# Scores of two heads at a time in the row halves of TensorE, and another order of the opening, in a layer of attention plus mixture of experts on one core

## The reference

```
x = L0_attn_x
xn = _layernorm(x, axis=-1)
x = x + attention(xn) + ffn(xn)

# attention: 16 heads of D = 8
qkv = x @ Wqkv + bqkv
q = q * cos + rotate_half(q) * sin           # k the same
scores = einsum('bhtd,bhsd->bhts', q, k) / sqrt(D)
probs = softmax(scores, axis=-1)
attn = einsum('bhts,bhsd->bhtd', probs, v) ; attn @ Wout + bout

# ffn: one shared and 16 routed experts of inner width 64, the best 2 of each token
router_logits = sigmoid(x @ gate_w + gate_b)
expert_values, expert_indices = top_k(router_logits, k=2)   # values divided by their sum
hg, hu = x @ experts_wg[e], x @ experts_wu[e]
out[e] = (silu(hg) * hu) @ experts_wd[e]
return x + shared_mlp(x) + sum of the 2 selected, weighted
```

## Time and profile before

| what | value |
|---|---|
| median of 3 runs | 251.86 us |
| the profiled execution | 251.57 us |
| its span, first to last instruction | 249.8 us (1.8 us lie around it) |
| PE / DVE / ACT / POOL busy | 215.1 / 186.4 / 141.6 / 173.0 us |
| granted clock of TensorE, mean | 0.963 of 2.4 GHz |
| DMA, mean | 106 GB/s |

### The profile page before, as it was taken

How to read it: one execution, slowest core, us unless ns; L and a number is a source line. 1 busy time by engine, 2 the same in 40 slices (tenths; PEclk the granted TensorE clock), 3 DMA queues, 4 the chain that set the end, 5 groups by cost and what they waited for, 6 DMA issues and landing times.

```text
span 249.8 us, 4841 instructions
## 1 busy us (share of the span) xinstructions
PE 215.1 (86%) x1612; PEld 140.1 (56%) x1612; DVE 186.4 (75%) x400; ACT 141.6 (57%) x266; POOL 173.0 (69%) x247
## 2 busy tenths in 40 slices
PE   0473399997898999999858999999999999999973
PEld 0341165564555666676634566676767656675541
DVE  5885929999787687899935787998688878774301
ACT  2455033235556856675267567656666757667761
POOL 9186646899966748979195768778876774558622
PEclk9995559999999999999999999999999999999999
DMA  6925628120354331320744070504553540211201
GB/s 221 368 40 164 204 63 203 36 76 12 111 173 128 109 96 53 107 45 20 217 143 140 3 192 5 145 0 134 155 147 106 171 133 22 85 53 37 86 3 42
DMA packets 35953, 26.53 MB, mean 106 GB/s; under 512 B 4236, under 2 KB 30156, under 8 KB 35916
## 3 DMA queue, kind: packets, MB, share of 16 engines
q1 hardware_dynamic: 35224, 25.30, 34.8%
q10 hardware_dynamic: 704, 0.92, 1.0%
HBM read 18.53 MB, written 7.47 MB: 104 GB/s over the span
## 4 chain that ended last, share of the span: by engine, by line
PE 48%; DVE 21%; POOL 11%; issue 6%; DMA 5%; ACT 4%; SPq 4%; POOLq 0%; DVEq 0%; ACTq 0%
PE PV L514 8%; DVE mx L886 5%; PE S2b L500 4%; PE S2a L500 3%; PE S1a L486 3%; PE S1b L486 3%; PE Y L373 3%; PE FB L373 3%; SPq L302 3%; PE FA L373 3%; DMA wbc<-route_w 3%; POOL hid_lo L1001 2%; PE FA L375 2%; PE FA L374 2%; PE FB L375 2%
## 5 line engine op out<-in xcount | busy, mean ns | idle before, releaser
L1001 POOL TENSOR_TENSOR hid_lo<-gu,hid_hi 128x512 fp32r<-128x512 f32 (+1 forms) x36 | 46.4, 1288 | 26.6 <-ACT hid_hi L694 26.6
L661 ACT ACTIVATE probs<-S2b 128x512 f32<-128x512 f32 x64 | 38.1, 596 | 28.3 <-PE S2b L500 28.2
L985 POOL TENSOR_TENSOR gu<-gu,wbc 128x512 f32<-128x512 f32 x32 | 41.0, 1282 | 13.2 <-DMA wbc<-route_w 9.6
L886 DVE TENSOR_REDUCE mx<-S1a 128x2 f32<-128x512 f32 x65 | 44.4, 683 | 7.3 <-PE S1a L486 7.3
L886 DVE TENSOR_REDUCE mx<-S1b 128x2 f32<-128x512 f32 x63 | 43.0, 683 | 7.3 <-PE S1b L486 7.2
L661 ACT ACTIVATE probs<-S2a 128x512 f32<-128x512 f32 x64 | 38.3, 599 | 11.7 <-PE S2a L500 9.6
L514 PE MATMUL PV<-probs,vx 128*32 128x256 f32 x512 | 34.9, 384 | 4.3 <-ACT probs L661 4.3
L694 ACT ACTIVATE hid_hi<-gu 128x512 fp32r<-128x512 f32 (+1 forms) x36 | 22.7, 632 | 24.6 <-POOL gu L985 23.1
L895 DVE SCALAR_TENSOR_TENSOR th<-th,FA 128x512 f32<-128x512 f32 (+1 forms) x36 | 24.5, 682 | 13.7 <-ACT th L673 13.2
L673 ACT ACTIVATE th<-FA 128x512 f32<-128x512 f32 (+1 forms) x36 | 21.5, 597 | 18.5 <-PE FA L375 18.2
L876 DVE TENSOR_TENSOR gu<-FB,th 128x512 f32<-128x512 f32 (+1 forms) x36 | 24.6, 683 | 5.5 <-PE FB L375 5.4
(11 more groups left out here) (129 smaller groups left out, 433.1 us busy)
## 6 DMA issues: line engine op xcount, KB each, us to landing
wbc<-route_w SPq DMA_DIRECT2D x64, 128.0 KB, 3.1
q_hat<-q_parts SPq DMA_DIRECT2D x32, 96.0 KB, 2.8
k_hat<-k_parts SPq DMA_DIRECT2D x32, 96.0 KB, 2.7
k_parts<-parts SPq DMA_DIRECT2D x8, 192.0 KB, 2.2
q_parts<-parts SPq DMA_DIRECT2D x8, 192.0 KB, 2.2
x_sb<-in_x SPq DMA_DIRECT2D x4, 256.0 KB, 4.0
q_parts<-parts SPq DMA_DIRECT2D x8, 128.0 KB, 2.1
k_parts<-parts SPq DMA_DIRECT2D x8, 128.0 KB, 2.1
```

The source lines that it names most:

```text
L661: nc.scalar.activation(probs[:, head % (2 * NQ), :], S2[head % 2][:], ACT.Exp, scale=SCALE).then_inc(exp_done, 1)
L886: nc.vector.tensor_reduce(mx[:, (q // QB) % 2, (q // 2) % 2, :, q % 2, i], S1[use % 2][:].rearrange("p (t s) -> p t s", t=SB), axis=AX.X, ...
L985: nc.gpsimd.tensor_tensor(gu[:, m % 2, :], gu[:, m % 2, :], wbc[:, g % 2, c - 1, :], ALU.mult).then_inc(gu_weighted, 1)
L1001: nc.gpsimd.tensor_tensor(hid_lo[0:rows, m % 2, :], gu[0:rows, m % 2, :], hid_hi[0:rows, m % 2, :].bitcast(f32), ALU.subtract).then_inc(hi ...
```

## The change

**Scores.** `q_hat` and `k_hat` keep the two heads of a pair in the two halves of the partitions: head r in rows 64r to 64r+47, its three rows of maxima or ones in 64r+48 to 64r+50. There are no zero rows, and both memsets go. `max_scores` and `exp_scores` now take two heads in one call, at steps i = 0 and 2, one head in each row half (`row_half`), and write the two banks in turn: four matmuls, over 48 rows or 51, with the heads alternating. They wait until both banks have been read. `load_max` is two DMAs, not one.

**Order in a block.** On PE `exp_scores` and `max_scores` stand together, `attend` goes to step 0 behind them and ahead of hg, and `maxima_to_rows` to the end of the even block, behind hu. ACT takes the exponentials ahead of the tanh of step 1, and `hid_hi` at step 3 behind all four. DVE takes th at step 1 behind two maxima. POOL takes the `hid_lo` of the chunk before ahead of the weighting `gu`, where it stood last in its block. SP issues `load_route` first in a block.

**Opening.** G1 of group 1 moves into block -5, behind G6; POOL's split of the second sequence is cut in two (blocks -6 and -5), and `wd_lo` in nine pieces, one to a block, for each of which `down` of the first group waits. DVE computes the variances of groups 2 and 3 ahead of the last split stage; SP issues the first two `load_route` ahead of the second sequence's `scratch`.

The diff, cut to its core:

```
-MROW = 2 * KROWS
+HROWS = 64
+KALL = KROWS + PARTS
 MROWS = 2 * PARTS
-KALL = MROW + MROWS
...
-    "G1": {2: 3, 3: 11},
+    "G1": {1: -5, 2: 3, 3: 11},
...
+    (0, 0, 1): -6, (0, 1, 1): -5,
...
+def row_half(q, i):
+    return (q + i) % 2
...
-                for r in range(2):  rows = slice(KROWS * r, KROWS * (r + 1))
+                for r in range(2):  rows = slice(HROWS * r, HROWS * r + KROWS)
...
             load_hats(1)
-            scratch(1)
             load_route(0, 0)
             load_route(0, 1)
+            scratch(1)
...
             for blk in range(FIRST, LAST + 1):
+                ahead = blk + CHLEAD + ROUTE_AHEAD
+                if 2 < ahead < NCHUNKS and ahead % NCH:
+                    load_route(ahead // NCH, ahead % NCH - 1)
                 if blk % 2 == 0 and blk // 2 + 3 in range(4, 2 * B):
                     load_hats(blk // 2 + 3)
...
+            def max_scores(q, first):
+                b, hg, slot = q // QB, (q // 2) % 2, (q // QB) % 2
+                if q % 2 == 0 and first == 0:
                     pe.wait_ge(hat_ld[(q // 2) % 4], 64 * (q // 8 + 1))
-                bank = take_s(("max", q * NQ + i))
+                banks = [take_s(("max", q * NQ + i)) for i in (first, first + 1)]
                 for t in range(SB):
+                    for i, bank in zip((first, first + 1), banks):
+                        r = row_half(q, i)
+                        rows, pair = slice(HROWS * r, HROWS * r + KROWS), NQ * hg + i
+                        last = nc.tensor.matmul(bank[:, t * T:(t + 1) * T], q_hat[rows, slot, pair, t * P:(t + 1) * P],
+                                                k_hat[rows, slot, pair, :], start=True, stop=True)
+                        if t == SB - 1:
+                            last.then_inc(s1_ready, 1)
...
+            def exp_scores(q, first):
                 if head >= 2:
-                    pe.wait_ge(exp_done, head - 1)
+                    pe.wait_ge(exp_done, head)
                 for s in range(SB):
+                    for i in (first, first + 1):
+                        r = row_half(q, i)
+                        rows, pair = slice(HROWS * r, HROWS * r + KALL), NQ * hg + i
+                        last = nc.tensor.matmul(S2[i % 2][:, s * T:(s + 1) * T], ...
...
                 pe.wait_ge(hid_ready, n + 1)
-                if n == 0:
-                    pe.wait_ge(down_split, 2)
+                if n < NCH:
+                    pe.wait_ge(down_split, n + 1)
...
-                    if i == 1 and 0 <= blk - 1 < NBLK:
-                        attend(blk - 1)
...
+                    if i % 2 == 0:
+                        if 0 <= blk < NBLK:
+                            exp_scores(blk, i)
+                        if 0 <= q < NBLK:
+                            max_scores(q, i)
+                    if i == 0 and 0 <= blk - 1 < NBLK:
+                        attend(blk - 1)
...
-                    if i == 0 and transposed_half(blk) is not None:
-                        maxima_to_rows(transposed_half(blk))
                     if i == 3 and n < NCHUNKS:
                         up(n, "hu")
+                    if i == 3 and negated_half(blk) is not None:
+                        maxima_to_rows(negated_half(blk))
...
-                    if i == 2 and 0 <= n - 1 < NCHUNKS:
+                    if i == 3 and 0 <= n - 1 < NCHUNKS:        # ACT, hid_hi
...
-            nc.vector.memset(k_hat[0:MROW, 0] ..., 0).then_inc(hat_zeroed, 1)
-            nc.gpsimd.memset(k_hat[0:MROW, 1] ..., 0).then_inc(hat_zeroed, 1)
...
+            variances([2, 3])
             for w in range(2):
                 dve.wait_ge(parts_done[0], 4)
                 split_stage(nc.vector, dve, 4, w, 0, 0).then_inc(parts_done[0], 1)
-            moments([3])
-            variances([2, 3])
...
+            def down_low(c):
+                rows = I if c == 0 else P
+                if c == 0:
+                    pool.wait_ge(down_hi_ready, 1)
+                nc.gpsimd.tensor_tensor(wd_lo[0:rows, c, :], wd_sb[0:rows, c, :], wd_hi[0:rows, c, :].bitcast(f32),
+                                        ALU.subtract).then_inc(down_split, 1)
...
+                if 0 <= m - 1 < NCHUNKS:                       # POOL, hid_lo of the chunk before
+                    pool.wait_ge(hid_hi_ready, m)
+                    nc.gpsimd.tensor_tensor(hid_lo[0:rows, (m - 1) % 2, :], ...).then_inc(hid_ready, 1)
                 if 0 <= m < NCHUNKS:
                     pool.wait_ge(fb_read, B_USE["hu", m] + 1)
...
+                if 0 <= m < NCH:
+                    down_low(m)
```

125 lines of the change are left out of this document (47 added, 78 removed).

## The result

The changed kernel takes 254.76 us (median of 4 runs, 254.35 to 255.84) and the kernel before 251.87 us (251.49 to 252.37) on the same chip: a ratio of 1.013 [1.0101, 1.0159], slower by 1.3%. The forecast was 237 us. The profiled spans are 252.6 and 249.8 us.

A forecast was written before the change was run, and what follows sets the result against it. The prediction took PE to bound batches 19 to 27 and nearly 3 to 19. It summed 251.57 - 3.0 - 9.3 - 1.7 - 0.3 = 237.3, said as 237 us, with a range of 230 to 246.5.

The forecast's parts named there:

- batches 3 to 19: Steady stretch: ten blocks at 59.7 us by POOL's load, six at 33.0, sum 92.7 for 102.02, so -9.3 us.
- POOL's roundtrip to ACT also goes, as hid_lo takes the chunk before: Batches 3 to 19: POOL's wait on ACT vanishes because hid_lo is made a chunk later; counted inside the -9.3 us.
- the ring: Loop of score pair, PV, hg, tanh, th and reduce: 4.9 us a block, above PE's plain 4.4; -1.7 from 19 to 27.
- ACT waits for POOL: Rival: POOL's weighting comes 1.23 us later, behind hid_lo, delaying ACT's hid_hi and exponentials; +17.2, 254.5 us; chance 0.06.
- the unloaded blocks: The other six blocks of batches 4 to 19, taken at PE's pace plus some loss: 5.5 us each, 33.0 us.
- Scores in pairs: PE's eight score matmuls take 0.48 instead of 0.92 us, twice a block: 0.88 saved, 0.3 back for layout changes.
- Row halves do not overlap: Rival: the eight matmuls of a pair gain nothing from two row halves; +0.44 twice a block, 252.9 us; chance 0.08.
- The opening: Up to batch 3: routing starts 2.8 us earlier, den 2.2 shorter, first negation 3.3 earlier at 42.2; gives -3.0 us.
- The balance of +0.3: Blocks -2 to 2: five wd_lo pieces of 0.35 us add 1.75, a 1.40 us wait for wbc goes.
- a clock under 1.00: Sign of being wrong: the clock falls in the steady stretch, as PE gets gaps it did not have.
- The wait for wbc of 4.76 us: POOL's wait for a routing weight that SP issues behind a scratch; it goes, counted inside -9.3 from 3 to 19.
- The ring and POOL add up: Rival: PE's ring waits make POOL start loaded blocks late without catching up; -4.4 from 3 to 19, 244 us; chance 0.22.

The follow-up runs named there:

- e9: Changed kernel with POOL's hid_lo ahead of the negation, wd_lo in two instructions behind chunk 0's weighting, third routing weight issued with the first two: 245.75 us.
- e1: Changed kernel with one swap on POOL, hid_lo of the chunk before ahead of the negation instead of behind it: 249.93 us.
- e12: e9 with POOL's hid_lo made on 128 of its 512 columns from chunk 4 on, the rest left out: 239.82 us.
- e3: Kernel before with the new opening alone, wd_lo in nine pieces included: 255.02 us.
- e7: e3 with wd_lo in two instructions behind chunk 0's weighting on POOL instead of nine pieces: 252.75 us.
- e8: e3 with SP issuing the third routing weight with the first two, ahead of the second scratch: 252.42 us.
- e10: Kernel before with the new opening and the edits of both e7 and e8: 250.5 us.
- e18: Changed kernel with SP's routing weights put back behind hats, max rows and scratch: 259.7 us.
- e13: e9 with the negation on DVE behind th of step 1, instead of at the head of POOL's even blocks: 260.25 us.
- e2: Changed kernel with hg ahead of PV (attend) in step 0 on PE: 254.46 us.
- e5: Changed kernel with the edits of e1 and e2 together: 249.95 us.
- e16: e9 with wd_lo times hid_hi left out of every down product on PE, two matmuls instead of three: 242.4 us.
- e15: e9 with the four matmuls of a score pair issued two of one half, then two of the other: 245.0 us.

## Why the prediction was wrong

By its own terms, in us of span:

```
                    forecast   changed   e9
up to batch 3         -3.0      -0.67   -5.13
batches 3 to 19       -9.3      +1.21   -0.51
batches 19 to 27      -1.7      +0.65   -0.56
batches 27 to 31      -0.3      +1.70   +0.33
behind batch 31        0        -0.09   -0.04
sum                  -14.3      +2.80   -5.91
```

**The step that failed first is "POOL's roundtrip to ACT also goes, as hid_lo takes the chunk before".** It was written as a gain, and the price of the new place was put at nothing: hid_lo now stands behind the negation, which waits for DVE's maxima. e1 puts it at 4.8 us. POOL's wait for ACT's hid_hi did fall, from 26.6 to 10.7 us, but in e1 it is back at 25.6 and the kernel is faster: the roundtrip was not what cost. The fault reaches the stretches that the forecast had for the ring and for ACT too, in e1 by 1.21 us from 19 to 27 and 1.35 from 27 to 31. The rival *ACT waits for POOL* gave 254.5 us, near the measured time, but by luck: ACT's wait fell to 11.7 us, and it was PE that waited.

**The mis-sized term is the unloaded blocks.** For the ten blocks with splits and their neighbours I forecast 30.5 + 29.2 = 59.7 us; they take 31.90 + 29.77 = 61.67. For the other six I had 33.0 at PE's pace; they take 13.48 + 22.12 + 5.96 = 41.56. Of the 10.5 us between 92.7 and 103.23 this is 8.6. The kernel before, cut as above, would have told: there the ten blocks took 61.75 and the six 12.69 + 20.86 + 6.72 = 40.27, 6.7 us each. I had divided 102.02 by 16 and taken the blocks without a split for the short ones, when they hold the residual, the waits for xT and the late routing weight. e1, without the negation ahead of hid_lo, brings the six to 13.52 + 19.19 + 6.27 = 38.98, so 2.6 of the 8.6 us are the first fault over again; e9 brings them to 11.88 + 19.17 + 6.30 = 37.35 (and its ten to 34.28 + 29.88 = 64.16, with the fallen clock of batch 9 to 10). The last 4.3 us above 33.0 are not shown to have one cause; in e12 the six take 36.15, so POOL holds part of them.

**Scores in pairs save less than I took, since single scores cost less.** I counted 16 x 0.115 = 1.84 us before, and 0.88 less 0.3 saved. The 0.115 was read within a run of score matmuls; beside a product two cost less. PE of the kernel before:

```profile
207.12 0.39 PE L500 MATMUL S2b<-q_hat,k_hat 102*128 102x256 bf16 x2
207.35 0.38 PE L486 MATMUL S1a<-k_hat,q_hat 96*128 96x256 bf16 x2
207.49 0.47 PE L373 MATMUL FB<-xT_hi,wu_hi 128*128 128x512 f32 x1
```

Four take 0.37 us (207.12 to 207.49), as the product starts 0.14 behind the last two. Eight behind PV took 0.81 us (205.54 to the product at 206.35 in the same timeline), so 16 cost 0.81 + 2 x 0.37 = 1.55, and 1.65 with the 0.1 into PV. PE of the changed kernel:

```profile
205.10 0.28 PE L508 MATMUL S2a<-q_hat,k_hat 51*128 51x256 bf16 x1
205.11 0.28 PE L508 MATMUL S2b<-q_hat,k_hat 51*128 51x256 bf16 x1
...
205.73 0.27 PE L490 MATMUL S1b<-k_hat,q_hat 48*128 48x256 bf16 x1 [0.24 <-DVE mx L891]
...
206.06 1.07 PE L523 MATMUL PV<-probs,vx 128*32 128x256 f32 x16
...
207.95 0.28 PE L508 MATMUL S2a<-q_hat,k_hat 51*128 51x256 bf16 x1
...
208.50 0.50 PE L374 MATMUL Y<-hid_hi,wd_hi 128*128 128x512 f32 x1
```

The eight at 207.95 take 0.55 to the product at 208.50, and the change of layout into them 0.1. The first four at 205.10 and the last four at 205.73 take 0.23 + 0.33 = 0.56 to PV, and again 0.1 into them: 1.31 in all. So the side after was nearly as forecast (0.96 and four changes, 1.36); the side before was 0.3 too dear. The saving is 0.34 us a block, not 0.58. Two things take it back. S1b at 205.73 starts 0.50 behind S2b at 205.23 and not 0.10, as it waits for the maxima (the ring). And in an even block the transposition now takes 0.21 us of PE with its own change of layout (210.12 to 210.33 in the same timeline), where before PV started 0.02 behind it (209.51 to 209.53). A plain block with it, and with 0.37 us of waiting for DVE's copy (S2b at 210.45, S1 at 210.93), is 5.19 us (206.06 to 211.25) for 4.99 before. That the halves overlap was right (0.01 us apart), and so the rival *Row halves do not overlap* was wrong, with its 252.9 us. The Trainium skill (TensorEngine Tiling (Array Packing), "Key Properties") was weighed for both halves: tiles at work in parallel and a drain at each change of mode. The traces now agree with both: starts 0.01 us apart, and about 0.1 us at each change.

**The opening.** The first negation was forecast for 42.2 and came at 42.59. The terms in front of it do not give 42.2 (4.5 us less some 2 given back is 2.5, and 3.3 was written; 2.94 came), so that it came near is in part luck. The balance of +0.3 behind it failed. I priced a piece at 2.81 / 8 = 0.35 and it takes 0.46; I let the wait of 1.40 us for wbc go, and another came at 46.66, since the third routing weight still stood behind the scratch and the hats. And I did not price the clock, though I had named a clock under 1.00 as a sign of being wrong: in e3 it falls behind the pauses that these make for PE (0.92 from batch 0 to 3). e3 shows the loss (3.9 us at batch 3), e7, e8 and e10 take it apart, and e9 shows that the lead then arrives.

**What was right.** The wait for wbc of 4.76 us, and that it would go (e18: 4.9 us). That a ring stands there: in e13 0.92 us more on DVE in it come out as 0.86. But its 4.9 us do not set the pace alone, as e2 and e5 show. *The ring and POOL add up* was the nearest rival in kind, and e12 and e16 show its pattern: of the work taken from one engine less than half comes back as time. It said 244; e9, which has the forecast's lag of hid_lo without its fault, has 245.75. The parts do not match, so the nearness is luck: the rival had -3.0 up to batch 3 and -4.4 from 3 to 19, e9 has -5.13 and -0.51.

What stays open: why the clock falls between batches 9 and 10 in e9, behind pauses of 0.92 and 0.46 us, and not in e1 behind the same ones, and how the rest of the stretch from 3 to 19 divides between the shared wait for both score banks and PV's place ahead of hg.

## What to carry to other kernels

A step that is moved on a queue inherits every wait that stands ahead of it: before a gain is written down, name the instruction that it now follows and whom that one waits for. A mean per block hides which blocks are slow, so cut the stretch at each kind of block first, and price a saving only in those where that engine ends last. An early start counts only if every input of the chain comes earlier too; look for the one with its own clock, here a weight behind other transfers on SP. And compare the granted clocks of two windows before their lengths: one block with a fallen clock made half of what two of the experiments seemed to show.

## What the runs showed of the hardware

- TensorE ran two row halves side by side whether their matmuls were issued in alternation or two by two: starts 0.01 us apart and the same time within the noise, 245.75 and 245.0 us (e9, e15).
- Two bfloat16 score matmuls right before a product of another kind took 0.14 us and not 0.23 (207.35 to 207.49): a cost read within a run of one kind was too high for a short run.
- After pauses of 2.4 (e3) and 3.1 us (the changed kernel) PE's matmuls of 512 columns started 0.43 us apart and not 0.23, for about 4 us: these pauses cost more than their length. Not every pause did: 2.25 us in the kernel before (up to PV at 126.80) and 1.70 in e1 (136.80) left the granted clock at 1.00, and in e9 it fell to 1.2 GHz behind 0.92 and 0.46 us.
- A DVE addition of 128x16 took 0.18 us with POOL out of the way, against 0.22 on POOL, but 0.67 and more beside some of POOL's operations: what small work costs on DVE depended on what POOL did (e13).
